# Adjacency tiles transposed by f32 products with a column of ones, loads moved ahead, more PSUM banks for attention's projections, and a norm in four parts

## The reference, cut to what matters

```python
h = jnp.maximum(_layernorm(x), 0.0)
x = x + L0(h, adj, adj, Wq, Wk, Wv, Wout)     # 8 heads; logits q k^T * scale + adj + adj, -1e6 where adj == 0
h = jnp.maximum(_layernorm(x), 0.0)
x = x + L1(h, adj, W1, W2, W3, U1, U2, U3, gamma, beta)
h = jnp.maximum(_layernorm(x), 0.0)
x = x + L2(h, adj, W, b)
h = jnp.maximum(_layernorm(x), 0.0)
x = x + L3(h, adj, weight)
```

## Time and profile before

| | us |
|---|---|
| runs | 3420.27, 3431.0, 3427.85 |
| median | 3427.85 |
| profiled execution, its own time | 3428.46 |
| its span (first to last instruction) | 3426.6 |
| mean granted TensorE clock | 0.935 of full |

### The profile page before, as it was taken

How to read it: one execution, slowest core, us unless ns; L and a number is a source line. 1 busy time by engine, 2 the same in 40 slices (tenths; PEclk the granted TensorE clock), 3 DMA queues, 4 the chain that set the end, 5 groups by cost and what they waited for, 6 DMA issues and landing times. The chain is left out here.

```text
span 3426.6 us, 57642 instructions
## 1 busy us (share of the span) xinstructions
PE 2910.1 (85%) x20376; PEld 2136.8 (62%) x20376; DVE 2201.0 (64%) x4355; ACT 1341.7 (39%) x1734; POOL 58.7 (2%) x68
## 2 busy tenths in 40 slices
PE   2469999999999999999999869778885668687599
PEld 1356676766767667676676537556654466576488
DVE  7965555556565555655656568888687887895430
ACT  4743434334434343443344333323326364632221
POOL 0000000000000000000000000000000000000110
PEclk7579999999999999999999979999987889899799
DMA  7946838468385683865838703010010010100500
GB/s 261 377 152 166 198 89 201 118 169 198 89 198 135 155 200 87 198 150 138 198 90 209 176 31 99 13 38 26 3 56 29 1 43 8 50 22 4 227 1 26
DMA packets 587856, 396.79 MB, mean 116 GB/s; under 512 B 538563, under 2 KB 553414, under 8 KB 562118
## 3 DMA queue, kind: packets, MB, share of 16 engines
q1 hardware_dynamic: 585990, 382.49, 41.4%
q10 hardware_dynamic: 1728, 12.58, 1.1%
HBM read 223.05 MB, written 37.75 MB: 76 GB/s over the span
## 5 line engine op out<-in xcount | busy, mean ns | idle before, releaser
L735 DVE SCALAR_TENSOR_TENSOR e_lo<-e,e_hi 128x2048 f16<-128x2048 f32 x128 | 293.3, 2292 | 441.5 <-ACT e_hi L657 441.5
L597 PE MATMUL av<-vw_hi,pT_hi 128*128 128x256 f16 x2048 | 559.5, 273 | 7.9 <-DMA pT_lo<-e_lo 7.9
L597 PE MATMUL av<-vw_lo,pT_hi 128*128 128x256 f16 x2048 | 559.5, 273 | 0.0
L597 PE MATMUL av<-vw_hi,pT_lo 128*128 128x256 f16 x2048 | 559.4, 273 | 0.0
L586 PE MATMUL logits<-kT_hi,qT_hi 128*128 128x512 f16 x1024 | 389.0, 380 | 9.2 <-DVE att_small L721 7.3
L586 PE MATMUL logits<-kT_lo,qT_hi 128*128 128x512 f16 x1024 | 388.1, 379 | 0.0
L586 PE MATMUL logits<-kT_hi,qT_lo 128*128 128x512 f16 x1024 | 388.1, 379 | 0.0
L651 ACT ACTIVATE att_small<-att_small,minus 128x1 f32<-128x1 f32 x128 | 37.7, 295 | 835.5 <-DVE att_small L730 835.5
L721 DVE CUSTOM_DVE_ANT_0 e<-logits,bias,att_small 128x1024 f32<-128x1024 f32 x256 | 328.6, 1283 | 1.0 <-issue 0.3
L1935 DVE SCALAR_TENSOR_TENSOR nuc_junk<-nuc_e,nuc_thr 128x2048 bf16<-128x2048 f32 x140 | 323.7, 2349 | 6.0 <-issue 2.2
L652 ACT ACTIVATE e<-e,att_small,sc 128x2048 f32<-128x2048 f32 x128 | 266.2, 2079 | 0.0
(11 more groups left out here) (401 smaller groups left out, 5797.6 us busy)
## 6 DMA issues: line engine op xcount, KB each, us to landing
bias<-bias_scratch SPq DMA_DIRECT2D x130, 1024.0 KB, 4.8
bias_scratch<-adj_bias SPq DMA_DIRECT2D x16, 1024.0 KB, 8.1
adjT_scratch<-adjT SPq DMA_DIRECT2D x16, 1024.0 KB, 7.4
nuc_at_hi<-adjT_scratch SPq DMA_DIRECT2D x32, 512.0 KB, 3.7
nuc_at_lo<-adjT_scratch SPq DMA_DIRECT2D x32, 512.0 KB, 4.5
adjT<-adjT_scratch SPq DMA_DIRECT2D x16, 1024.0 KB, 19.9
adj_rows<-in_adj_dram ACTq DMA_DIRECT2D x12, 1024.0 KB, 9.2
adj_rows<-in_adj_dram SPq DMA_DIRECT2D x4, 1024.0 KB, 7.9
```

The source lines that it names most:

```text
L597: last = nc.tensor.matmul(AV[par][:, :], PT[par][w][:, m, :], VW[x][:, m, :], start=(m == 0 and w == x == 0), stop=(m == T - 1 and w == 1))
L735: nc.vector.scalar_tensor_tensor(out=EL[:, :], in0=E[par][:, :], scalar=P_SCALE, in1=EH[:, :], op0=ALU.mult, op1=ALU.subtract).then_inc(lo ...
```

## The change: what it does

1. **Loads.** The four `adj_rows` buffers live over setup and adjacency, and their first loads are issued by SP in setup, behind the loads of the weights.
2. **Transposes.** PE multiplies each block by `ident1`, the 128 x 128 identity with a 129th column of ones, as a plain f32 matmul instead of a transpose. The 129th column of the result is the column sum. The tile is cut in groups of 6, 6 and 4 blocks; there are four PSUM slots of two banks.
3. **DVE and ACT on them.** The reduces go; DVE copies the sums (a few elements) and makes the low part in two pieces a group. ACT makes the high part in three pieces instead of two.
4. **attend.** Groups 0 and 1 of `project(h, 0)` go into the banks of `vw_ps` and don't wait for the logits' readers; groups 4 and 5 then find their banks free. `project(h, 3)` rotates over three banks, the third of which is that of `av0`. The loops over the two halves of n = 0 and n = 3 are written out.
5. **refresh.** Statistics, power and centring go in four quads of four tiles; ACT does the scale and bias in the relu itself, so DVE's 16 passes (L1412) go. The wait for the small weights (L1415) now stands behind the first quad's statistics.

```diff
@@ setup, SP
+                for u in range(ADJ_AHEAD):
+                    sp.dma_start(adj_rows[u][:, :], adjacency_rows(a["adj"])[u // 2, u % 2, :, :]).then_inc(adj_here[u], 16)
                 sp.wait_ge(extremes, 1)
@@ adjacency
-        TP = [ps(c, f"adj_tp{q}", [P, N]) for q in range(2)]
+        TP = [ps(c, f"adj_tp{q}", [P, 2 * BANK]) for q in range(4)]
+        ident1 = sb(c, "ident_one", [P, P + 1])
+        FREE, TP_FREE = 2, 4
+        GROUPS = ((0, 6), (6, 6), (12, 4))
-                for u in range(AHEAD):
-                    sp.dma_start(A[u][:, :], rows[u // 2, u % 2, :, :]).then_inc(loaded[u], 16)
@@ PE
-                        for h in range(2):
-                            pe.wait_ge(lo_done, 2 * n + h + 1)
-                            for t in range(T // 2 * h, T // 2 * (h + 1)):
-                                last = nc.tensor.transpose(TP[q][:, t * P:(t + 1) * P], rows_u[...], ident[:, :])
+                        for g, (first, count) in enumerate(GROUPS):
+                            pe.wait_ge(lo_done, PER_TILE * n + g + 1)
+                            for b in range(count):
+                                o = slot(u, g)[:, place(g, b):place(g, b) + P + 1]
+                                last = nc.tensor.matmul(o, rows_u[...], ident1[:, :], start=True, stop=True)
                             last.then_inc(tposed, 1)
@@ DVE
-                            nc.vector.tensor_reduce(col[...], TP[q][...], X, ALU.add)
-                            nc.vector.scalar_tensor_tensor(out=half(AT[q][:, 1, :, :], h), in0=TP[q][...], ...)
+                            nc.vector.tensor_copy(col[:, first:first + number, ds(n, 1)]..., columns(u, g)[:, :, :, P:P + 1])
+                            for x in range(2):
+                                last = nc.vector.scalar_tensor_tensor(
+                                    out=blocks(AT[q][:, 1, :, :], g)[:, x, :, :], in0=columns(u, g)[:, x, :, 0:P], ...)
@@ attend, PE
+                                if j == 2:
+                                    pe.wait_ge(av_free, T * h - 1 + AV_FREE)
+                                pe.wait_ge(vw_free, PER_VW * h + VW_FREE + max(j - 2, 0))
-                                    o = VP[b % 2][:, m * D:(m + 1) * D]
+                                    o = VW_RING[j % 3][:, m * D:(m + 1) * D]
+                                if n == 0 and u == 0 and b == EARLY:
+                                    pe.wait_ge(logits_read, 32 * h + READS_FREE)
+                                if n == 0 and b < EARLY:
+                                    pe.wait_ge(bank_free, KQV * h + BANKS_FREE)
-                                    o = bank[b][:, m * ROWS:(m + 1) * ROWS]
+                                    o = (VP[b] if early else bank[b])[:, m * ROWS:(m + 1) * ROWS]
@@ refresh, ACT
-                            nc.scalar.activation(dst[:, t, :], dst[:, t, :], ACT.Relu).then_inc(ready, 1)
+                            nc.scalar.activation(dst[:, t, :], src[:, t, :], ACT.Relu, bias=minus[:, t:t + 1], scale=rstd[:, t:t + 1]).then_inc(ready, 1)
@@ refresh, DVE
+                    stats_of(0)
+                    v.wait_ge(w_loaded, 16 * 5)
+                    nc.vector.tensor_scalar(w3[:, :, :, :], w3[:, :, :, :], 0.5, None, ALU.mult).then_inc(halved, 1)
+                    for b in range(1, QUADS):
+                        stats_of(b)
+                        centre(b - 1)
+                    centre(QUADS - 1)
```

More of the change, by code:

```diff
@@ L50 @@
 P_NUC = 0.9
+ADJ_AHEAD = 4
 G = 4
@@ L144, in build @@
         gb = sb(g, "gamma_beta", [P, 2, D])
+        rows_here = [nc.alloc_semaphore(f"adj_rows_here{u}") for u in range(ADJ_AHEAD)]
         with ExitStack() as c:
@@ L150, in build @@
             hT_lo = sb(c, "hT_lo", [P, KC, N], F16)
-            phase(setup, a, bias_d, acc, ident, am, winv, sc, halfp, WH, WL, hT_hi, hT_lo)
-            phase(adjacency, a["adj"], bias_d, at_d, sc, ident, deg, row_mask)
+            with ExitStack() as c1:
+                rows = [sb(c1, f"adj_rows{u}", [P, N]) for u in range(ADJ_AHEAD)]
+                phase(setup, a, bias_d, acc, ident, am, winv, sc, halfp, WH, WL, hT_hi, hT_lo, rows, rows_here)
+                phase(adjacency, a["adj"], bias_d, at_d, sc, ident, deg, row_mask, rows, rows_here)
             phase(attend, a["L0_gnn_Wout"], bias_d, acc, ident, winv, sc, WH, WL, hT_hi, hT_lo, row_mask,
@@ L309, in adjacency @@
     at_stored = [sem(f"at_stored{q}") for q in range(2)]
-    rows = adj.rearrange("(q p c) m -> c q p m", q=2, p=P, c=CH)
-    AHEAD = 4
-    HALF = N // 2
+    rows = adjacency_rows(adj)
+    AHEAD = ADJ_AHEAD
     with ExitStack() as c:
-        A = [sb(c, f"adj_rows{u}", [P, N]) for u in range(AHEAD)]
         W = [sb(c, f"adj_permuted{q}", [P, N]) for q in range(2)]
@@ L345, in _ @@
             def _(pe):
+                pe.wait_ge(dve, 2)
                 with pe.Fori(0, T // AHEAD) as i:
@@ L368, in tile @@
                     s.wait_ge(at_stored[q], 16 * turn + 16)
-                    for h in range(2):
-                        s.wait_ge(tposed, 2 * n + h + 1)
-                        nc.scalar.activation(half(AT[q][:, 0, :, :], h), TP[q][:, HALF * h:HALF * (h + 1)], ACT.Copy,
+                    for g in range(PER_TILE):
+                        s.wait_ge(tposed, PER_TILE * n + g + 1)
+                        nc.scalar.activation(blocks(AT[q][:, 0, :, :], g), columns(u, g)[:, :, :, 0:P], ACT.Copy,
                                              scale=A_SCALE).then_inc(hi_done, 1)
@@ L403, in _ @@
                                                        op0=ALU.mult, op1=ALU.add, accum_out=count[:, ds(n, 1)]).then_inc(made, 1)
[L404 to L412, removed]
+                        for g, (first, number) in enumerate(GROUPS):
+                            v.wait_ge(hi_done, PER_TILE * n + g + 1)
+                            nc.vector.tensor_copy(col[:, first:first + number, ds(n, 1)].rearrange("p (a b) n -> p a b n", a=2),
+                                                  columns(u, g)[:, :, :, P:P + 1])
+                            for x in range(2):
+                                last = nc.vector.scalar_tensor_tensor(
+                                    out=blocks(AT[q][:, 1, :, :], g)[:, x, :, :], in0=columns(u, g)[:, x, :, 0:P],
+                                    scalar=A_SCALE, in1=blocks(AT[q][:, 0, :, :], g)[:, x, :, :], op0=ALU.mult, op1=ALU.subtract)
+                            last.then_inc(lo_done, 1)
+                link = Chain(v, dve, 2)
+                v.wait_ge(lo_done, PER_TILE * T + TP_FREE)
                 nc.vector.tensor_reduce(deg[:, 1, :], col[:, :, :], X, ALU.add).then_inc(summed, 1)
@@ L573, in project @@
                             last.then_inc(proj, 1)
+                    if n == 3:
+                        pe.wait_ge(wo_hi_s, h + 1)
+                        pe.wait_ge(wo_lo_s, h + 2)
+                    if n in (0, 3):
+                        half(0)
+                        half(1)
+                    else:
+                        with pe.Fori(0, 2) as u:
+                            half(u)
                 def qk(i, t, first=None):
@@ L659, in evacuate, with half @@
                 def evacuate(h, n):
-                    with s.Fori(0, 2) as u:
+                    def half(u):
                         for b in range(4):
@@ L664, in evacuate @@
                             nc.scalar.activation(to[0], source, ACT.Copy, scale=VW_SCALE if n == 3 else 1.0).then_inc(proj_hi, 1)
+                    if n in (0, 3):
+                        half(0)
+                        half(1)
+                    else:
+                        with s.Fori(0, 2) as u:
+                            half(u)
                 def begin(h):
@@ L750, in evacuate, with half @@
                 def evacuate(h, n):
-                    with v.Fori(0, 2) as u:
+                    def half(u):
                         for b in range(4):
```

111 lines of the change are left out of this document (73 added, 38 removed).

## The result

The changed kernel takes 3375.91 us (median of 4 runs, 3374.33 to 3377.64), beside 3427.97 for the kernel before: a ratio of 0.9852, with a 95% interval of 0.9835 to 0.9869. The forecast was 3378.7.

What follows compares the result with a forecast made beforehand. DVE was taken to set adjacency's pace with the DMAs close behind, and PE to run through most of attention. Gains of 21 (adjacency), 25.8 (attention) and 3.0 us (refresh) sum to 49.8: 3428.46 - 49.8 = 3378.7, range 3364 to 3398.

Steps and rivals of the forecast that it cites:

- The price of a product: Adjacency, PE: a 129-column product costs 0.44 us at 1.2 GHz, 0.22 at 2.4; a tile's 16 cost 7.0 or 3.5.
- The doubling in line 1595's rows: PE: f32 instructions take 592 ns for 512 columns, f16 380; so each passes twice and each product four times.
- The bound: Adjacency: PE stays behind the others; nine tiles take 7.5 us by the DMAs, six 6.8, the first 8.0.
- PE becomes the bound: Rival, adjacency: four transposes a product at 1.2 GHz, 14.1 us a tile, 86 us longer, 3486 us in all; chance 0.03.
- The DMAs: Adjacency: transfers of 3.15 MB a tile at 426 to 427 GB/s take 7.4 us, taken as 7.5; stage gains 21 us.
- DVE's tile: Adjacency: DVE's work without the reduces, with smaller low parts and three small copies, sums to 6.8 us a tile.
- The start: Adjacency: with the first rows loaded in setup, DVE's first tile starts at 62.6 instead of 67.17, 4.6 us earlier.
- early start and groups: Attention, between heads: groups 0 and 1 start at once and later groups follow sooner; 1.4 us a boundary.
- the gap before group 6: Attention, between heads: PE still waits there for the third emptied bank, a gap of 1.7 us.
- a rival let PE fetch more instructions: Rival, attention: written-out loops cost instruction fetches or a later wait takes the banks' gain; 3400 us, chance 0.05.
- the third slot: Attention, projection 3: three banks cover the wait for an emptied bank, so 96 matmuls run through; 1.9 us a boundary.
- Refresh: Refresh: working in quads lets PE's first transpose start 3.2 us earlier; taken as 3.0 us, ends 2 and 4.5.

Runs made afterwards that it cites:

- mixed run: Changed kernel with the third group of each adjacency tile made by transposes and its column sums by a DVE reduction: 3369.8 us, ratio 0.9838.
- combined kernel: Changed kernel with third group by transposes, an extra unread POOL power in attention, and refresh's halving of small weights moved behind the first centring: 3368.64 us, ratio 0.9832.

## Why the prediction was right, and where it was not

Two of its steps failed, in opposite directions, and the total was right by that, which was luck.

**The price of a product** is the step that failed in adjacency: "a 129-column product then is two instructions of what one transpose takes". The count of instructions was right, their size wrong. In the changed kernel each takes 0.240 us at the high clock; a transpose takes 0.22 at half the clock, so 0.11 at the full one, and 0.11 apart they come in part of the third groups of the mixed run. That is 4.4 transposes a product; the forecast had two. The doubling in line 1595's rows said that the moving data pass twice in each instruction, and that was taken for all of it. The products' records show 337 ns for a weight load and 405 for a matmul, of which 0.240 us remain from one to the next. The likely reason, which no run isolates, is that with only 129 columns to move the load of the weights counts, while in line 1595's rows, with 512, it doesn't show. The Trainium skill's factor of 4 (TensorE: Matmul & The Clock Gate, Terms), which the prediction set aside, agrees with the trace but for a tenth: 4.4.

**The bound** followed from it. The forecast had PE hidden behind transfers of 7.5 us a tile; PE needs 7.68, and is the bound by 0.2 to 0.4 us a tile over what comes next (over tiles 4 to 15 the run with the third group by transposes has 7.4 us a tile, the one with all by transposes 7.3). So the nine tiles forecast at 7.5 came out near it for another reason, and the six forecast at 6.8 took 7.7 too; those six are 5.3 of the 7.3 us that the tiles took more than forecast. The run without later loads and the run with transposes show it from both sides. The rival "PE becomes the bound" was right in its mechanism and wrong in its clock: PE, never idle, ran at a granted clock of 1.00, 2.4 GHz, and not at 1.2. The prediction had the number, "even four would give 7.0 us, hidden"; 7.68 was not hidden.

**The DMAs** were forecast well: with PE out of the way the stage ends where the forecast put it, within 0.3 us, at 415 GB/s. The 358 GB/s that the Trainium skill gives (DMA: Bandwidth & Descriptors, Specifications) doesn't agree with the rows of 409 to 419 GB/s over 65 us. DVE's tile was forecast at 6.8 us and has 6.5, the three small copies taking 0.07 us each behind other work, not 0.17. The start, 4.6 against 4.4, held, and the run with late loads prices part 1 at 4.3.

**Between heads,** what the prediction worked out was right: early start and groups 1.4 (1.42), the gap before group 6 of 1.7 (1.5), no gap in projection 3. What it left out was the loops. It held the written-out projections for neutral or harmful (a rival let PE fetch more instructions), and they gave 2.68 us a head, more than either of the two mechanisms. Of the 1.9 put down to the third slot, 0.84 is the slot's and 1.0 the loop's. Over all eight heads it is 20.2 us of the attention in the trace of the run that only writes out, whose time is 3404.91 beside 3426.13. In head 0 the third slot was undersized too (some 4 us of the 7.2).

A written-out projection pauses less because each of the three hand-offs of a bank is shorter by 0.10 to 0.15 us, and the register instruction that stood in each of them is gone. The semaphores, their values' order and the slots are the same. What isn't shown is why the loop over the items, whose own instructions are the same, also pauses less behind a written-out projection 3 (0.26 us once and 0.04 at each of 13 pauses).

**Refresh** was oversized: 3.0 against 2.1. That the first quad's power "is done by 1970.3" assumed that POOL answers at once. Before, the first power ran 7.0 us after the phase's first statistics, 0.3 us after it was asked, so its trace couldn't show whether POOL would have been ready sooner. In the changed kernel it came 7.2 us after, 5.2 after it was asked. The operation of another kind that POOL ran before it is the reduction over partitions, at 250 us. In the combined kernel the extra power right behind that reduction pays instead, 7.1 us where nobody waits, and in refresh the answer comes in 0.1 us. The Trainium skill (GPSIMD Engine Reference, Instruction dispatch) says that the first call of newly loaded POOL code costs some 6 us without an instruction in the profile; these rows agree in kind, with 7.1 us. DVE's wait for the small weights, 2.3 us, was forecast (2.7).

**The 3.5 us lost afterwards** need no cause in the change: the second profile of the same kernel has them back and 3.6 us more, with the clock at 0.95 in place of 0.93 in L1's first step. Phases whose instructions nobody touched differ by up to 9 us between the profiles (487.7 to 496.5 from refresh to refresh in the kernel before and in the one with the new attention alone). A single profile of this kernel can't price anything behind 1960 us to better than that, so a small effect of the change there isn't ruled out either. Before it, the same code gives the same head's period within 0.1 us, and a first head within 1.5.

## What to carry to other kernels

Where two resources are both at a share of 1.00, take work away from one and leave the other: a third of the bytes gone and 0.2 us gained, the products made cheap and 8.1, told in two runs what the profile could not. Price an f32 product by weights and data together, from a row with as few columns as the one to be added, before using it to take a reduction off DVE; and mix the two ways if either engine alone is near its limit. Try a short loop around waits written out by itself, on all the engines that hand the buffer on: here it was worth more than the extra buffers that came with it.

## What the runs showed of the hardware that was not expected

- An f32 product of 128 x 128 weights and 129 columns costs 0.48 us at the full clock, 4.4 f32 transposes of the same block.
- A loop of two turns on PE, ACT and DVE around groups that wait costs 0.33 to 0.36 us at each pause in it, 0.10 to 0.15 at each engine's hand-off, where a register instruction stands behind the wait: 2.68 us of a 217.5 us period for two such loops, 0.5% of the kernel's time in all.
- POOL's first power in refresh began 7.0 us into the phase when it was asked at 6.7, and 7.2 when it was asked at 2.0, 5.2 us late; one power run earlier behind the reduction over partitions took that to 0.1 us.
- The DMA engines held 409 to 419 GB/s over 65 us, with loads and stores mixed (three kernels).
- The clock granted in one unchanged stretch of 455 us was 0.93 in one execution of a kernel and 0.95 in the next.
